# A broadcast matmul issued one projection unit later, and VectorE's next low weights ahead of the copy of its result

## Chip, cores, metric

The kernel runs on one core of a Trainium2 chip. The metric is the device time of one execution in microseconds; lower is better. The core's engines are TensorE (PE; its weight loads are listed as PEld), VectorE (DVE), ScalarE (ACT), GpSimd (POOL), and SyncE (SP), which here issues the DMAs.

## What is computed

One decoder layer on x (2 x 256 x 512, float32): attention with 32 heads of 128, a product with a quantised context, and a feed-forward part with a low-rank mixture. Only the attention's projections matter here:

```python
q = hidden_states @ Wq + bq
k = hidden_states @ Wk + bk
v = hidden_states @ Wv + bv
q = rms_norm(q, gq)      # over all 4096 columns, before the heads are split
k = rms_norm(k, gk)
...
attn = softmax(einsum('bhqd,bhkd->bhqk', q, k) / sqrt(128))
```

`rms_norm(x, w)` is `w * x * rsqrt(mean(x*x) + 1e-6)`. The mean runs over the 4096 columns of one token, so no key can be normalised until all 32 heads of keys are projected.

## The kernel before

The 512 tokens (T) stand along the free dimension, and the model's 512 columns lie in 4 chunks of 128 partitions. To keep float32's accuracy with TensorE's faster float32r matmuls, each operand is split into a high and a low part: the high part is a cast by ScalarE, the low part is the operand minus its high part. A product is three matmuls: high by high, low by high, high by low.

**Projection units.** One head of keys or queries is one unit. `project(i, r, before)` (line 476) is unit u = before + 4i + r; keys are units 0 to 31 (before = 0), queries units 32 to 63 (before = NH = 32). A unit is 12 matmuls (4 chunks by 3) of 128x512 into one of two PSUM banks: `p_flat[2]` (the profile calls it p_t) for even units, `p_flat[3]` (p_o) for odd ones. It waits for its low weights (`w_lo_dve`, line 480) and, for its bank, until the squares of the unit two before are taken (line 482).

**The feeding of a unit.**
- SyncE loads the head's weights into one of four slots of `raw` (line 322) once `w_lo_dve` says that the slot is free.
- ScalarE casts them to `w_hi` (`weights_hi`, line 695). There are two weight buffers, so it waits until unit u - 2 is finished (`proj_ready`, line 694). Then it takes a finished unit out of PSUM (`take`): with its bias into `k_all` or `q_all` (line 709), and squared into `square` (line 710).
- VectorE makes `w_lo` = `raw` - `w_hi` (`weights_lo`, line 1080).
- GpSimd adds the squares into `acc_k` or `acc_q` (`add_square`, line 929).

**The norms of the keys.** After unit 33 TensorE sums `acc_k` over the partitions with eight small matmuls (`sum_squares`, line 501) into `p_flat[0]` (p_v). VectorE scales them (`mean_squares`, line 1156), GpSimd takes the power -0.5 into `rk_t` (line 937). VectorE writes four diagonal tiles `diag` (line 1164), and TensorE multiplies `ones` with them (line 524) into `p_flat[1]` (p_s), which puts every token's factor on all partitions. VectorE copies this to `rkb` (line 1167). Then `norm_k` (line 1085) multiplies each head of `k_all` by its gain and by `rkb`.

**The order of the work** is the order of the instructions written out for each engine; every engine works through its own list, and semaphores hold it at the waits. VectorE's list around the change: `weights_lo` for units 32, 33, 34; `mean_squares`; the four `diag`; `weights_lo` for unit 35; the wait for `rkb_ready` and the copy to `rkb`; then, for units 36 to 39, `weights_lo` and two `norm_k` behind each (head r and head 4 + r); from unit 40 on one `norm_k` for each unit. TensorE's list: units 32 and 33, `sum_squares`, unit 34, the wait for `diag_made` and the broadcast matmul, unit 35, then a loop over units 36 to 63.

Behind the projections stands a loop over 16 pairs of heads: scores, softmax, the values' projection and the output projection, woven together in the same way; behind it the quantised product and the feed-forward part.

Of the kernel before, what the change touches and what calls it, by code (L numbers as in the profile page):

```python
# [33 lines left out]
NH, DH = 32, 128  # L34
# [14 lines left out]
def decoder_layer(nc, x, ctx_t, wk, wq, wv, wo, bk, bq, bv, bo, gk, gq, qscal, ra_w, base_b, router_b, bm_w,  # L49
                  expert_map, out):  # L50
    st = ExitStack()
    with st:
        def sem(name):
            return st.enter_context(nc.semaphore(name))
# [18 lines left out]
        def here(name, shape, dt, at=None):  # L73
            return place(name, shape, dt, at)[0]
# [50 lines left out]
        rkb = here("rkb", [P, T], F32, vl_at + half)  # L125
# [60 lines left out]
        p_flat = [p_v[:].rearrange("p a b -> p (a b)"), p_s[:].rearrange("p a b -> p (a b)"),  # L186
                  p_t[:].rearrange("p a b -> p (a b)"), p_o[:]]
# [22 lines left out]
        rkb_ready = sem("rkb_ready")  # L210
# [73 lines left out]
        def peeled(n, first, end):  # L284

            return isinstance(n, int) and first <= n < end

        def head(a, h):

            return a[:, bass.ds(h, 1), :].rearrange("p a t -> p (a t)")  # L290

        def column(a, h):
            return a[:, bass.ds(h, 1)]

        def parts(n):

            return [w[:, n, 0:NC * DH].rearrange("p (c n) -> p c n", c=NC) for w in (w_hi, w_lo)]
# [165 lines left out]
        def _(pe):  # L463
# [12 lines left out]
            def project(i, r, before):  # L476

                u = before + 4 * i + r
                n = r % 2
                pe.wait_ge(w_lo_dve, u + 1)  # L480
                if not peeled(u, 0, 2):
                    pe.wait_ge(squared, u - 1)
                hi, lo = parts(n)
                for c in range(NC):
                    pe.matmul(p_flat[2 + n], hi[:, c, :], xnt_hi[:, c, :], start=(c == 0), stop=False)  # L485
                    pe.matmul(p_flat[2 + n], lo[:, c, :], xnt_hi[:, c, :], start=False, stop=False)  # L486
                    if not peeled(u, 0, 1):
                        mm = pe.matmul(p_flat[2 + n], hi[:, c, :], xnt_lo[:, c, :], start=False,  # L488
                                       stop=(c == NC - 1))
                if peeled(u, 0, 1):  # L490
                    pe.wait_ge(xt_lo, NT)
                    for c in range(NC):
                        mm = pe.matmul(p_flat[2 + n], hi[:, c, :], xnt_lo[:, c, :], start=False,
                                       stop=(c == NC - 1))
                mm.then_inc(proj_ready, 1)

            def sum_squares(sums, dst, n):

                pe.wait_ge(summed, n)
                for t in range(NT):  # L500
                    mm = pe.matmul(dst[:, t:t + 1], sums[:, t * P:(t + 1) * P], ones[:, 0:1],
                                   start=True, stop=True)
                mm.then_inc(ssq_ready, 1)
# [7 lines left out]
            for r in range(4):  # L511
                pe.wait_ge(xb_lo_done, r + 1)
                for part in (xb_hi, xb_lo):
# [6 lines left out]
            project(0, 1, NH)  # L520
            sum_squares(acc_k, p_flat[0], NH)
            project(0, 2, NH)
            pe.wait_ge(diag_made, NT)
            pe.matmul(p_flat[1], ones[:], diag[:].rearrange("p t n -> p (t n)"), start=True, stop=True
                      ).then_inc(rkb_ready, 1)
            project(0, 3, NH)
            with pe.Fori(1, NH // 4) as i:
                for r in range(4):
                    project(i, r, NH)
# [491 lines left out]
        def _(dve):  # L1021
            links = 0

            def link(ins):

                nonlocal links
                links += 1
                ins.then_inc(chain, 1)
                dve.wait_ge(chain, links)
# [47 lines left out]
            def weights_lo(i, r, before):  # L1077
                dve.wait_ge(w_hi_done, before + 4 * i + r + 1)
                n = r % 2
                dve.tensor_tensor(w_lo[:, n, 0:NC * DH], raw[:, r, :], w_hi[:, n, 0:NC * DH], ALU.subtract  # L1080
                                  ).then_inc(w_lo_dve, 1)

            def norm_k(i, r):
                h = 4 * i + r
                dve.scalar_tensor_tensor(out=head(k_all, h), in0=head(k_all, h), scalar=column(g_c, h),
                                         in1=rkb[:], op0=ALU.mult, op1=ALU.mult).then_inc(k_normed, 1)
# [76 lines left out]
            for t in range(NT):  # L1163
                dve.tensor_scalar(diag[:, t, :], ident[:], rk_t[:, t:t + 1], None, ALU.mult).then_inc(diag_made, 1)
            weights_lo(0, 3, NH)
            dve.wait_ge(rkb_ready, 1)
            link(dve.tensor_copy(rkb[:], p_flat[1]))
            for r in range(4):
                weights_lo(1, r, NH)
                norm_k(0, r)  # L1170
                norm_k(1, r)
            with dve.Fori(2, NH // 4) as i:
# [289 lines left out]
```

## Time and profile before

| | us |
|---|---|
| median of 3 runs | 540.79 |
| the runs | 540.56, 540.79, 543.37 |
| the profiled execution, its own time | 541.91 |
| its span, first to last instruction | 540.1 |

Busy time of the engines in that span: TensorE 524.2 us (97%), ScalarE 355.6 (66%), VectorE 330.3 (61%), GpSimd 269.9 (50%). Times inside the profile are counted from the start of the span. The profiled execution took 1.8 us more than its span, and 1.1 us more than the median of the runs. In a row of a timeline stand the start, the duration, engine, line, operation, output<-inputs, shape and count; in brackets the idle time of the engine before it and what ended it.

### The profile page before, as it was taken

Reading aid. Unit: us, or ns where it says so; the run is one execution under the profiler, and the core shown is the slowest. Engines: PE = TensorE matmul, PEld = TensorE weight load, DVE = VectorE, ACT = ScalarE, POOL = GpSimd, SP = SyncE. Lnnn points to the kernel's source line nnn. Section 1 sums busy time; section 2 is a strip of 40 time slices with the busy share of each in tenths; the row PEclk is TensorE's granted clock in tenths of the full one; section 3 lists DMA queues with packets and bytes.
Section 4 is the critical chain, followed back from the end, with each engine's and each line's share of the span. In section 5 each row is a group of like instructions: output and inputs, shape, how many; then the busy total and the mean of one; then the engine's idle time right before and its main releaser. Section 6 shows DMA issues by size and latency. Waiting matters only on the chain.

```text
span 540.1 us, 9859 instructions
## 1 busy us (share of the span) xinstructions
PE 524.2 (97%) x3246; PEld 464.5 (86%) x3246; DVE 330.3 (61%) x695; ACT 355.6 (66%) x745; POOL 269.9 (50%) x229
## 2 busy tenths in 40 slices
PE   6999999989999999999999999999999999999887
PEld 6888888868888889999999999999999999986486
DVE  6254444287555567666766666666666666666665
ACT  3566666546666667767777777767767776776730
POOL 3344444355444446564646555464646556465340
PEclk9999999999999999999999999999999999999999
DMA  5344735323333321222122111121142311220002
GB/s 181 130 138 130 231 94 172 97 60 97 97 97 97 78 80 41 58 60 59 58 58 58 51 53 51 58 58 58 58 120 65 124 50 57 59 79 19 1 1 79
DMA packets 23351, 43.43 MB, mean 80 GB/s; under 512 B 3616, under 2 KB 3616, under 8 KB 23072
## 3 DMA queue, kind: packets, MB, share of 16 engines
q1 hardware_dynamic: 23328, 43.13, 26.7%
q8 instruction: 13, 0.21, 0.2%
q14 instruction: 10, 0.08, 0.0%
HBM read 41.03 MB, written 2.10 MB: 80 GB/s over the span
## 4 chain that ended last, share of the span: by engine, by line
PE 72%; issue 9%; POOL 8%; DVE 5%; ACT 3%; DMA 1%; POOLq 0%; SPq 0%; ACTq 0%; DVEq 0%
POOL acc_k L929 7%; PE p_v L564 5%; PE p_v L566 5%; PE p_v L565 5%; PE acc L583 5%; PE acc L584 5%; PE acc L585 5%; PE p_t L550 5%; PE p_o L602 3%; PE p_o L604 3%; PE p_o L486 3%; PE p_o L603 3%; PE p_o L485 3%; PE p_o L488 3%; PE p_s L543 3%
## 5 line engine op out<-in xcount | busy, mean ns | idle before, releaser
L1080 DVE TENSOR_TENSOR w_lo<-raw,w_hi 128x512 fp32r<-128x512 f32 x64 | 44.2, 691 | 82.1 <-ACT w_hi L695 82.1
L947 POOL TENSOR_TENSOR wo_lo<-raw,wo_hi 128x512 fp32r<-128x512 f32 x31 | 40.0, 1290 | 100.2 <-ACT wo_hi L829 100.2
L695 ACT CAST w_hi<-raw 128x512 fp32r<-128x512 f32 x64 | 39.9, 623 | 70.0 <-PE p_o L488 32.8
L764 ACT ACTIVATE probs<-p_s,nbias,rq_t 128x256 f32<-128x256 f32 x128 | 71.2, 562 | 19.2 <-DVE nbias L1182 19.2
L564 PE MATMUL p_v<-w_hi,xnt_hi 128*128 128x256 f32 x256 | 77.3, 302 | 0.0
L566 PE MATMUL p_v<-w_hi,xnt_lo 128*128 128x256 f32 x256 | 72.3, 283 | 0.0
L565 PE MATMUL p_v<-w_lo,xnt_hi 128*128 128x256 f32 x256 | 72.3, 282 | 0.0
L929 POOL TENSOR_TENSOR acc_k<-acc_k,square 128x512 f32<-128x512 f32 x32 | 41.6, 1300 | 53.5 <-ACT square L710 53.5
L929 POOL TENSOR_TENSOR acc_q<-acc_q,square 128x512 f32<-128x512 f32 x32 | 42.7, 1334 | 43.1 <-ACT square L710 42.8
L813 ACT CAST pt_hi<-p_t 128x512 fp32r<-128x512 f32 x64 | 37.3, 583 | 38.4 <-PE p_t L550 38.4
L947 POOL TENSOR_TENSOR w_lo<-raw,w_hi 128x512 fp32r<-128x512 f32 x32 | 44.9, 1404 | 20.6 <-ACT w_hi L747 20.6
L1180 DVE TENSOR_REDUCE nmax<-p_s 128x2 f32<-128x512 f32 x64 | 43.9, 686 | 14.5 <-PE p_s L543 13.6
L485 PE MATMUL p_t<-xnt_hi,w_hi 128*128 128x512 f32 x128 | 50.1, 391 | 0.7 <-ACT xnt_hi L719 0.7
L583 PE MATMUL acc<-wo_hi,o_hi 128*128 128x512 f32 x124 | 49.4, 398 | 1.0 <-POOL wo_lo L947 0.6
L485 PE MATMUL p_o<-xnt_hi,w_hi 128*128 128x512 f32 x128 | 50.2, 392 | 0.0
L486 PE MATMUL p_t<-xnt_hi,w_lo 128*128 128x512 f32 x128 | 49.9, 390 | 0.0
L488 PE MATMUL p_o<-xnt_lo,w_hi 128*128 128x512 f32 x128 | 49.8, 389 | 0.0
L486 PE MATMUL p_o<-xnt_hi,w_lo 128*128 128x512 f32 x128 | 49.8, 389 | 0.0
L564 PEld LDWEIGHTS p_v<-w_hi,xnt_hi 128*128 128x128 f32 x256 | 48.8, 191 | 0.3 <-issue 0.2
L584 PE MATMUL acc<-wo_hi,o_lo 128*128 128x512 f32 x124 | 49.0, 395 | 0.0
L565 PEld LDWEIGHTS p_v<-w_lo,xnt_hi 128*128 128x128 f32 x256 | 48.9, 191 | 0.0
L566 PEld LDWEIGHTS p_v<-w_hi,xnt_lo 128*128 128x128 f32 x256 | 48.7, 190 | 0.0
(263 smaller groups left out, 1500.9 us busy)
## 6 DMA issues: line engine op xcount, KB each, us to landing
raw<-in_wv SPq DMA_DIRECT2D x36, 256.0 KB, 2.6
raw<-in_wk SPq DMA_DIRECT2D x32, 256.0 KB, 2.6
raw<-in_wq SPq DMA_DIRECT2D x32, 256.0 KB, 2.6
raw<-in_wo SPq DMA_DIRECT2D x31, 256.0 KB, 2.6
ctx_f<-in_ctx SPq DMA_DIRECT2D x4, 512.0 KB, 3.6
xin<-in_x SPq DMA_DIRECT2D x4, 256.0 KB, 3.7
xb<-in_x SPq DMA_DIRECT2D x4, 256.0 KB, 5.9
ctx_kept<-ctx_k SPq DMA_DIRECT2D x1, 1024.0 KB, 5.0
```

Source lines behind the costliest of these rows:

```text
L485: pe.matmul(p_flat[2 + n], hi[:, c, :], xnt_hi[:, c, :], start=(c == 0), stop=False)
L486: pe.matmul(p_flat[2 + n], lo[:, c, :], xnt_hi[:, c, :], start=False, stop=False)
L488: mm = pe.matmul(p_flat[2 + n], hi[:, c, :], xnt_lo[:, c, :], start=False, stop=(c == NC - 1))
L564: pe.matmul(p_v[:, t % 2, :], xnt_hi[:, c, tt], hi[:, c, :], start=(c == 0), stop=False)
L565: pe.matmul(p_v[:, t % 2, :], xnt_hi[:, c, tt], lo[:, c, :], start=False, stop=False)
L566: mm = pe.matmul(p_v[:, t % 2, :], xnt_lo[:, c, tt], hi[:, c, :], start=False, stop=(c == NC - 1))
L583: pe.matmul(acc[t][:], oh[:, tt], wh[:], start=False, stop=False, skip_group_check=True)
L584: pe.matmul(acc[t][:], ol[:, tt], wh[:], start=False, stop=False, skip_group_check=True)
L764: act.activation(probs[:, b, a, :], p_s[:, a, :], ACT.Exp, bias=nbias[:, b, a:a + 1], scale=rq_t[:, 2 * b + a:2 * b + a + 1], accum_out=rs ...
L929: pool.tensor_tensor(sums[:], sums[:], square[:, r % 2, :], ALU.add).then_inc(summed, 1)
L947: pool.tensor_tensor(dst, raw[:, slot, :], hi, ALU.subtract).then_inc(w_lo_pool, 1)
L1080: dve.tensor_tensor(w_lo[:, n, 0:NC * DH], raw[:, r, :], w_hi[:, n, 0:NC * DH], ALU.subtract).then_inc(w_lo_dve, 1)
```

## The change

TensorE issues unit 35 (`project(0, 3, NH)`) ahead of the wait for the diagonal tiles and the broadcast matmul, instead of behind them. VectorE makes the low weights of unit 36 ahead of the wait for the broadcast matmul's result and of its copy, instead of behind them. The first two `norm_k` stay behind the copy. All else is as it was, VectorE's order of `diag` and the low weights of unit 35 included.

```diff
@@ -520,10 +520,10 @@
             project(0, 1, NH)
             sum_squares(acc_k, p_flat[0], NH)
             project(0, 2, NH)
+            project(0, 3, NH)
             pe.wait_ge(diag_made, NT)
             pe.matmul(p_flat[1], ones[:], diag[:].rearrange("p t n -> p (t n)"), start=True, stop=True
                       ).then_inc(rkb_ready, 1)
-            project(0, 3, NH)
             with pe.Fori(1, NH // 4) as i:
                 for r in range(4):
                     project(i, r, NH)
@@ -1163,10 +1163,11 @@
             for t in range(NT):
                 dve.tensor_scalar(diag[:, t, :], ident[:], rk_t[:, t:t + 1], None, ALU.mult).then_inc(diag_made, 1)
             weights_lo(0, 3, NH)
-            dve.wait_ge(rkb_ready, 1)
-            link(dve.tensor_copy(rkb[:], p_flat[1]))
             for r in range(4):
                 weights_lo(1, r, NH)
+                if r == 0:
+                    dve.wait_ge(rkb_ready, 1)
+                    link(dve.tensor_copy(rkb[:], p_flat[1]))
                 norm_k(0, r)
                 norm_k(1, r)
             with dve.Fori(2, NH // 4) as i:
```

## Rows read from the trace of the kernel before

**Rows 1.** The page: TensorE's busy time, the chain's shares, the query weights' DMAs

```profile
PE 524.2 (97%) x3246; PEld 464.5 (86%) x3246; DVE 330.3 (61%) x695; ACT 355.6 (66%) x745; POOL 269.9 (50%) x229
...
PE 72%; issue 9%; POOL 8%; DVE 5%; ACT 3%; DMA 1%; POOLq 0%; SPq 0%; ACTq 0%; DVEq 0%
...
raw<-in_wq SPq DMA_DIRECT2D x32, 256.0 KB, 2.6
```

**Rows 2.** Windows: length, busy (count) of PE, PEld, DVE, ACT, POOL; clock, DMA, GB/s

```profile
116.00:190.00 74.00, 74.00 (x328) 61.31 (x327) 42.56 (x58) 49.54 (x84) 35.91 (x27) 1.00 0.33 92
206.00:510.00 304.00, 300.29 (x2136) 275.95 (x2134) 205.11 (x466) 220.72 (x513) 168.12 (x138) 1.00 0.20 60
```

**Rows 3.** TensorE's timeline: broadcast, unit 35's first matmuls, starts of units 36 and 37

```profile
112.28 1.13 PE L524 MATMUL p_s<-diag,ones 128*128 128x512 f32 x2 [1.41 <-DVE diag L1164]
112.88 0.75 PE L485 MATMUL p_o<-xnt_hi,w_hi 128*128 128x512 f32 x1
113.47 0.40 PE L486 MATMUL p_o<-xnt_hi,w_lo 128*128 128x512 f32 x1
...
116.00 0.39 PE L485 MATMUL p_t<-xnt_hi,w_hi 128*128 128x512 f32 x1
...
118.72 0.39 PE L485 MATMUL p_o<-xnt_hi,w_hi 128*128 128x512 f32 x1
```

**Rows 4.** VectorE's timeline, from the diagonals to the low weights of unit 38 and the norms behind

```profile
109.31 2.91 DVE L1164 TENSOR_SCALAR diag<-ident,rk_t 128x128 f32<-128x128 f32 x4 [1.14 <-POOL rk_t L937]
112.14 0.68 DVE L1080 TENSOR_TENSOR w_lo<-raw,w_hi 128x512 fp32r<-128x512 f32 x1
113.44 0.69 DVE L1167 COPY rkb<-p_s 128x512 f32<-128x512 f32 x1 [0.62 <-PE p_s L524]
114.17 0.69 DVE L1080 TENSOR_TENSOR w_lo<-raw,w_hi 128x512 fp32r<-128x512 f32 x1
114.78 1.41 DVE L1085 SCALAR_TENSOR_TENSOR k_all<-k_all,g_c,rkb 128x512 f32<-128x512 f32 x2
116.86 0.69 DVE L1080 TENSOR_TENSOR w_lo<-raw,w_hi 128x512 fp32r<-128x512 f32 x1 [0.67 <-ACT w_hi L695]
117.47 2.45 DVE L1085 SCALAR_TENSOR_TENSOR k_all<-k_all,g_c,rkb 128x512 f32<-128x512 f32 x2
119.84 0.68 DVE L1080 TENSOR_TENSOR w_lo<-raw,w_hi 128x512 fp32r<-128x512 f32 x1
120.44 2.44 DVE L1085 SCALAR_TENSOR_TENSOR k_all<-k_all,g_c,rkb 128x512 f32<-128x512 f32 x2
```

**Rows 5.** Waits of the weight loads, 106 to 131 us (total, times, longest)

```profile
PEld p_o L485 <- DVE w_lo L1080: 0.3, 1, 0.3
```

**Rows 6.** TensorE's timeline: the first three matmuls after an idle spell elsewhere

```profile
204.14 0.35 PE L602 MATMUL p_o<-pt_hi,v_hi 128*128 128x256 f32 x1 [0.64 <-DVE pt_lo L1249]
204.33 0.28 PE L603 MATMUL p_o<-pt_hi,v_lo 128*128 128x256 f32 x1
204.45 0.28 PE L604 MATMUL p_o<-pt_lo,v_hi 128*128 128x256 f32 x1
```

**Rows 7.** ScalarE's timeline: the high weights of units 35, 36 and 37

```profile
107.28 0.62 ACT L695 CAST w_hi<-raw 128x512 fp32r<-128x512 f32 x1 [0.93 <-PE p_o L488]
...
110.90 0.62 ACT L695 CAST w_hi<-raw 128x512 fp32r<-128x512 f32 x1 [1.83 <-PE p_t L488]
...
116.20 0.62 ACT L695 CAST w_hi<-raw 128x512 fp32r<-128x512 f32 x1 [3.52 <-PE p_o L488]
```

**Rows 8.** GpSimd's timeline: the squares of units 35 and 36

```profile
118.06 1.30 POOL L929 TENSOR_TENSOR acc_q<-acc_q,square 128x512 f32<-128x512 f32 x1 [4.03 <-ACT square L710]
120.86 1.47 POOL L929 TENSOR_TENSOR acc_q<-acc_q,square 128x512 f32<-128x512 f32 x1 [1.50 <-ACT square L710]
```

**Rows 9.** Lines 1216 and 1217: count, duration in ns (min/median/max), first and last start

```profile
L1216 DVE TENSOR_TENSOR k_lo<-k_all,k_hi x1: 684/684/684, 191.5 to 191.5; 128x512 fp32r<-128x512 f32 x1
L1217 DVE TENSOR_TENSOR q_lo<-q_all,q_hi x1: 1783/1783/1783, 192.1 to 192.1; 128x512 fp32r<-128x512 f32 x1
```

## The prediction, made before the change was run

> **What bounds the kernel now.** I read the page first: TensorE (PE) is busy for 524.2 us of a span of 540.1, and it has by far the largest share of the chain that ended last [rows 1]. So a microsecond that TensorE loses is a microsecond of the span, unless a later wait swallows it. The windows say where such a wait could be: from 116 to 190 us TensorE is busy for all 74.00 us, and from 206 to 510 us for 300.29 of 304 [rows 2]. The rest of the kernel is fed by TensorE's own results, so nothing downstream has a date of its own; I take it that a delay at 116 us goes through to the end whole.
>
> Next I read TensorE's timeline around the edit [rows 3]. I number projection units from 0: units 0 to 31 are keys, 32 to 63 queries; `project(0,2,NH)` is unit 34 and `project(0,3,NH)` unit 35. After unit 34 TensorE idles 1.41 us until the diagonal tiles are made, and at 112.28 the broadcast matmul (line 524) starts, recorded as two of 1.13 us together. Unit 35 is issued at 112.88, but its second matmul follows only at 113.47, one pitch of 0.23 after the first really streams; so the first streams at 113.24. From there unit 36 begins 2.76 later, at 116.00, and units follow each other by 2.72 (116.00, 118.72). That 1.41 us is the only idle time that the edit can aim at.
>
> Then the other queues. VectorE makes the four diagonal tiles from 109.31 to 112.22 and, **behind them**, the low weights of unit 35 from 112.14 to 112.82 [rows 4]. The waits of the weight loads show one of 0.3 us, unit 35's, and it is for these low weights [rows 5]: they are ready just when TensorE asks, and no earlier.
>
> **What the change does, part by part.**
>
> *The broadcast matmul goes behind unit 35.* The wait for the diagonals leaves the front of unit 35. But unit 35 waits for w_lo of unit 35, and the diff leaves VectorE's order of diagonals, then w_lo(35), untouched. The wait does not go away; what is late next is w_lo(35). TensorE starts at 112.88 instead of 112.28 (from end of w_lo at 112.82 the 0.06 us seen before). The same matmuls are issued behind either start: one broadcast and unit 35, which took 116.00 − 112.28 = 3.72 us. So unit 36 starts at 112.88 + 3.72 = 116.60: **+0.60 us**. In other words the broadcast matmul used to run beside VectorE's w_lo(35), and loses that cover. Should the order matter for the matmul's price, 112.28 to 113.24 bounds it at 0.96 us with the restart; a restart costs some 0.07 (after an idle spell the first two matmuls start 0.19 apart, the next 0.12 [rows 6]), so I take 0.89 in mid-stream, between 0.8 and 1.1, the term moving with it between +0.5 and +0.8.
>
> *VectorE's w_lo(36) ahead of the copy.* It was made from 114.17 to 114.86 and needed at 116.00 [rows 3, 4]. Now it is made before the copy, with the high weights cast at 110.90 [rows 7]. It had 1.1 us of slack, so its gain is nothing. Without this edit it would sit behind the late copy, and that would cost; it only keeps its cover.
>
> *What now queues behind the late result.* The broadcast starts at 116.60 − 0.89 = 115.71. The copy used to start 1.16 after a start from idle, so 1.09 without the restart: 116.80. On VectorE, behind this wait, stand the copy, two norm_k and then w_lo(37), which unit 37 needs. Before, w_lo(37) was made at 116.86 ahead of its own two norms and needed at 118.72. Now: copy 116.80, first norm 0.73 later at 117.53, the second 0.66 later. If nothing disturbed them, w_lo(37) would run from 118.85 to 119.53, and TensorE, through with unit 36 at 116.60 + 2.72 = 119.32, would wait for 0.34 with signal and restart.
>
> They are disturbed. Two norms took 1.41 us at 114.78 and 2.45 at 117.47, where GpSimd's sum of squares ran from 118.06 to 119.36; the norms ended 0.56 after it [rows 4, 8]. At 120.44 the same again: GpSimd starts at 120.86, ends 1.14 after the first norm, at 122.33, and the second norm ends 0.55 later. So they take turns, whole instructions at a time. The subtraction at line 1217, of the same form as w_lo (a tensor minus another, both in SBUF), took 1783 ns where its neighbour at line 1216 took 684 [rows 9]. The Trainium skill, GPSIMD Engine Reference, Key points, says that GpSimd shares its SBUF interfaces with VectorE and contends with VectorE instructions that have two SBUF inputs. The trace agrees; norms and w_lo are all of that kind.
>
> Where is GpSimd now? ScalarE's cast of the high weights starts 0.20 after a unit ends, and GpSimd 1.86 after the cast (116.20 and 118.06) [rows 7, 8]. Unit 35 ends at 115.71, cast 115.91, GpSimd at 117.77, inside the first norm (117.53 to 118.28). GpSimd takes the next turn and ends at 119.42, the second norm at 119.98, w_lo(37) runs from 119.90 to 120.58, and unit 37 starts at 120.71 (0.06 and 0.07 more) instead of 119.32: **+1.39 us**. If GpSimd wins the first turn, all end the same.
>
> *The next round.* Unit 38 is wanted at 123.43. Norms at 120.50 and 121.16 to 121.91; unit 36 ended at 119.32, so GpSimd comes at 121.38, inside the second norm, and ends at 121.91 + 1.14 = 123.05. w_lo(38) ends at 123.61, unit 38 starts at 123.74: **+0.31 us**. It is nothing if VectorE keeps the turn. For w_lo(39) the cast waits for unit 37 (ends 123.43), GpSimd comes at 125.49, and w_lo(39), from 124.86 to 125.54, is ahead of it and needed at 126.46. From unit 40 on there is one norm per unit, and the delay stops growing.
>
> *Queues passed.* No DMA is moved. The load into the raw slot that w_lo(37) frees is issued 3 us later (120.6 for 117.5); it takes 2.6 us [rows 1] and is cast for unit 41 only when unit 39 ends, near 129.2. Cover of 6 us.
>
> **Sum:** 0.60 + 1.39 + 0.31 = 2.30 us. The profiled execution took 541.91 us with its span of 540.1; the sum on it gives 544.2. It stands 1.1 above the median of the runs, 540.79; on that, 543.1 us, 0.43% slower. About 0.5% (2.7 us) is what a measurement of this kernel can tell from no change.
>
> **The rivals.**
>
> *No turns taken, or fewer.* For it: w_lo itself has never met GpSimd in the projection loops, and the second turn rests on 0.2 us of timing. Then the terms are 0.60 + 0.34, or the third is nothing: 0.9 to 2.0 us, 541.7 to 542.8. Against it: both norms of rows 4 were held each time. Chance 0.24.
>
> *A third round: slower by over 0.5%.* VectorE's queue is fuller than TensorE's in units 37 to 39: w_lo(37) and w_lo(38) were made 2.98 us apart before (116.86, 119.84 [rows 4]) against units of 2.72, so it loses ground each round. If GpSimd's turn falls ahead of w_lo(39) instead of behind it, that ends at 126.77 + 0.56 = 127.33 and unit 39 starts at 127.46 for 126.46: one us more, 3.3 in all, 544.1. It decides where w_lo(39) starts after 125.49; I have it 0.6 earlier. Chance 0.18.
>
> *The change does what it says.* Unit 35 starts behind unit 34 and the 1.41 us go. It needs w_lo(35) made by 110.87, where the 1.41 us of idle time begin. Its high weights are cast by 107.9 [rows 7], so it could have been; but it stands behind the diagonals in the program, and VectorE works in order. The gain would be 1.41, 539.4, still within 0.5%. Chance 0.04.
>
> **How the numbers follow.** Forecast 0.54, rivals 0.24, 0.18, 0.04. The range 541.3 to 544.4 takes in the small case nearly whole and the third round. Within 0.5%: 0.54 + 0.24 + 0.04 = 0.82, of which 0.02 go to slower (the broadcast at its upper bound) and 0.01 to faster, so 0.79; slower 0.18 + 0.02 = 0.20; faster 0.01.
>
> **What would show it.** In the changed profile: TensorE idle about 2 us before unit 35, released by w_lo and not by the diagonals; the broadcast behind unit 35; VectorE's copy near 116.8; a second wait for w_lo of about 1.3 us before unit 37 and perhaps a third, small, before unit 38; norms of 1.78 us beside GpSimd's sums. The forecast is wrong if unit 35 starts near 110.9, if unit 37 starts without a wait, or if waits go on after unit 38; and also if TensorE's granted clock falls below the full value it holds throughout now [rows 2].

## The result, and the profile after

The changed kernel takes 544.86 us in the median of 14 runs (542.81 to 548.59), the kernel before 541.54 in the median of 14 (540.52 to 543.98). The ratio is 1.0063 with a 95% interval of 1.0041 to 1.0085: slower, by about 3.3 us. The forecast was a ratio of 1.0043 (2.30 us, 543.1), likeliest within 0.5%, with a range that ended at 544.4. So the direction was right and the size too small by 1 us. The median lies outside the range by 0.5 us. Of its distance to the forecast, 0.75 us come from the median of before, now 541.54 for 540.79: counted from the new median, the range would end at 545.15 and hold the result. The ratio does not depend on that, and it is above the 0.5% within which the forecast had it.

The profiled execution took 544.50 us with a span of 542.7. TensorE's timeline around the change (the lines that answer to [rows 3]); units 34 and 35, the broadcast, and the first matmuls of units 36 to 39:

```profile
106.38 0.49 PE L485 MATMUL p_t<-xnt_hi,w_hi 128*128 128x512 f32 x1
...
111.42 0.50 PE L485 MATMUL p_o<-xnt_hi,w_hi 128*128 128x512 f32 x1 [2.01 <-DVE w_lo L1080]
111.76 0.39 PE L486 MATMUL p_o<-xnt_hi,w_lo 128*128 128x512 f32 x1
...
112.74 0.63 PE L488 MATMUL p_o<-xnt_lo,w_hi 128*128 128x512 f32 x1
113.17 0.63 PE L485 MATMUL p_o<-xnt_hi,w_hi 128*128 128x512 f32 x1
...
115.72 1.17 PE L525 MATMUL p_s<-diag,ones 128*128 128x512 f32 x2
116.33 0.79 PE L485 MATMUL p_t<-xnt_hi,w_hi 128*128 128x512 f32 x1
...
120.84 0.49 PE L485 MATMUL p_o<-xnt_hi,w_hi 128*128 128x512 f32 x1 [1.23 <-DVE w_lo L1080]
...
123.80 0.50 PE L485 MATMUL p_t<-xnt_hi,w_hi 128*128 128x512 f32 x1
...
126.67 0.39 PE L485 MATMUL p_o<-xnt_hi,w_hi 128*128 128x512 f32 x1
```

The first wait is now 2.01 us, in front of unit 35, and what ends it is w_lo and not the diagonals. The second, of 1.23, stands in front of unit 37. Unit 38 begins 0.32 after the last matmul of unit 37 was issued at 123.48, instead of 0.23: the third, small one. All three were forecast. But look at the durations within unit 35. They are 0.39 at first and 0.63 from the sixth matmul on, and the starts stand 0.43 apart where they stood 0.23. The windows say why (columns as in [rows 2]):

```profile
109.40:111.40 2.00, 0.01 (x1) 0.00 (x0) 2.00 (x4) 1.78 (x3) 1.18 (x2) 1.00 0.00 0
111.40:112.40 1.00, 0.98 (x4) 0.85 (x5) 0.57 (x1) 0.00 (x0) 1.00 (x1) 1.00 0.00 0
112.40:115.70 3.30, 3.30 (x9) 2.52 (x9) 0.00 (x0) 0.00 (x0) 0.71 (x1) 0.53 0.56 159
115.70:117.00 1.30, 1.30 (x5) 0.75 (x4) 0.07 (x1) 1.04 (x2) 0.00 (x0) 0.88 0.00 0
```

From 112.4 to 115.7 TensorE's granted clock is 0.53 of full, that is, the lower level of 1.2 GHz nearly all the time. Finer windows put the fall at 112.6, 1.2 us **after** the idle spell, while TensorE was busy again, and the return at 116.0, some 3.4 us later. The Trainium skill, TensorE: Matmul & The Clock Gate, Part 1, says that the chip gates TensorE's clock to half according to how busy the engine has been; the trace agrees.

VectorE's timeline (for [rows 4]) and GpSimd's (for [rows 8]) show the turns:

```profile
107.86 2.91 DVE L1164 TENSOR_SCALAR diag<-ident,rk_t 128x128 f32<-128x128 f32 x4 [1.14 <-POOL rk_t L937]
110.69 1.28 DVE L1080 TENSOR_TENSOR w_lo<-raw,w_hi 128x512 fp32r<-128x512 f32 x2
116.94 0.69 DVE L1170 COPY rkb<-p_s 128x512 f32<-128x512 f32 x1 [4.96 <-PE p_s L525]
117.66 2.45 DVE L1085 SCALAR_TENSOR_TENSOR k_all<-k_all,g_c,rkb 128x512 f32<-128x512 f32 x2
120.04 0.68 DVE L1080 TENSOR_TENSOR w_lo<-raw,w_hi 128x512 fp32r<-128x512 f32 x1
120.64 1.40 DVE L1085 SCALAR_TENSOR_TENSOR k_all<-k_all,g_c,rkb 128x512 f32<-128x512 f32 x2
121.96 1.78 DVE L1080 TENSOR_TENSOR w_lo<-raw,w_hi 128x512 fp32r<-128x512 f32 x1
```

```profile
117.83 1.74 POOL L929 TENSOR_TENSOR acc_q<-acc_q,square 128x512 f32<-128x512 f32 x1 [4.71 <-ACT square L710]
121.60 1.60 POOL L929 TENSOR_TENSOR acc_q<-acc_q,square 128x512 f32<-128x512 f32 x1 [2.03 <-ACT square L710]
```

VectorE is idle 4.96 us for the broadcast. Then the two norms cost 2.45 beside GpSimd's sum, w_lo(37) ends at 120.72, and TensorE goes on at 120.84. In the next round it is w_lo(38) itself that is held, 1.78 us for 0.68: a w_lo had never met GpSimd in the projection loops of before, and it is held as line 1217 was.

**How the delay adds up.** The starts of the two executions differ (unit 34 began at 107.84 before and at 106.38 now, since the first unit began 1.4 us earlier), so I measure from the start of unit 34. To the start of unit 39 it was 124.16 − 107.84 = 16.32 us; now it is 126.67 − 106.38 = 20.29, 3.97 more. The forecast has 2.30 of it. Eight matmuls from 112.46 to 115.72 took 3.26 us for 8 x 0.227 = 1.81, so 1.45 more, and the broadcast some 0.1 more: the clock has the rest.

The 14 runs say the same. Those with a mean granted clock of 1.000 took 542.81, 543.17 and 543.17 us; at 0.996 to 0.997 the runs took 543.7 to 544.9, at 0.993 up to 545.7, at 0.987 to 0.990 548.0 to 548.6. A mean does not say where in the kernel the clock was low; the traces below show two more places.

### The profile page after: what moved, and what is told of

It is laid out like the page before. It is cut to its first block, busy times and chain, and to the rows that moved or that the text cites. A ratio compares the mean times of both kernels' runs of the same rounds, so it can differ in the third digit from the quotient of the medians.

```text
span 542.7 us, 9856 instructions
## 1 busy us (share of the span) xinstructions
PE 524.9 (97%) x3244; PEld 464.1 (86%) x3246; DVE 329.0 (61%) x695; ACT 355.6 (66%) x745; POOL 271.0 (50%) x229
## 4 chain that ended last, share of the span: by engine, by line
PE 71%; issue 9%; POOL 8%; DVE 6%; ACT 3%; DMA 1%; POOLq 0%; SPq 0%; ACTq 0%; DVEq 0%
POOL acc_k L929 7%; PE p_v L564 5%; PE p_v L566 5%; PE p_v L565 5%; PE acc L583 5%; PE acc L584 5%; PE acc L585 5%; PE p_t L550 5%; PE p_o L485 3%; PE p_o L488 3%; PE p_o L602 3%; PE p_o L486 3%; PE p_o L604 3%; PE p_o L603 3%; PE p_s L543 3%
## 5 line engine op out<-in xcount | busy, mean ns | idle before, releaser
L1080 DVE TENSOR_TENSOR w_lo<-raw,w_hi 128x512 fp32r<-128x512 f32 x64 | 45.3, 709 | 81.7 <-ACT w_hi L695 81.7
L929 POOL TENSOR_TENSOR acc_q<-acc_q,square 128x512 f32<-128x512 f32 x32 | 43.8, 1370 | 45.9 <-ACT square L710 45.6
```

The costliest lines, as they stand in the source:

```text
L929: pool.tensor_tensor(sums[:], sums[:], square[:, r % 2, :], ALU.add).then_inc(summed, 1)
```

## The experiments

The yardstick in the traces is the time from the start of unit 34 to the start of unit 41, 21.76 us before (129.60 − 107.84), or to unit 39, 16.32. It leaves the start and the tail of the kernel out.

**The changed kernel again**, on another chip, as it is:

> The changed kernel once more, beside the two above on the same chip. My account: its fastest runs, at clock 1.000, at 543.1 us (before + 2.3); the others, at 0.987 to 0.997, up to 5 us more; median 544.5 to 545. Rival, that the earlier runs were a property of their chip: median at 543 and no low clocks.

Median 544.59 us of 6 runs (543.55 to 545.04), ratio 1.0058 (1.0035 to 1.0080), 3.5 us above the 541.07 of before beside it. One run had clock 1.000, with 543.55. Its profile fell on a run in which the clock held in this stretch, and so shows the queue's part alone: TensorE waits 2.01 and 1.18 us, and unit 41 begins 24.14 us after unit 34, **2.38 more than before, against 2.30 forecast**. The trace with the fallen clock has 20.29 to unit 39, this one 18.70: 1.59 us for one fall of the clock.

```profile
111.48 0.50 PE L485 MATMUL p_o<-xnt_hi,w_hi 128*128 128x512 f32 x1 [2.01 <-DVE w_lo L1080]
...
114.34 1.02 PE L525 MATMUL p_s<-diag,ones 128*128 128x512 f32 x2
...
119.30 0.49 PE L485 MATMUL p_o<-xnt_hi,w_hi 128*128 128x512 f32 x1 [1.18 <-DVE w_lo L1080]
```

**The idle spell filled.** Eight matmuls with nothing to do, in front of unit 35; their bank is overwritten by the broadcast:

```diff
             project(0, 2, NH)
+            for _ in range(8):
+                pe.matmul(p_flat[1], ident_r[:], xnt_hi[:, 0, :], start=True, stop=True)
             project(0, 3, NH)
```

> The changed kernel, with 8 matmuls of 128x512 put into TensorE's idle spell of 2.0 us before unit 35 (8 x 0.227 = 1.8 us, results overwritten by the broadcast). Theory that the missing 1.5 us are TensorE's clock, fallen to half after that spell: the granted clock is 1.000 in nearly all runs, unit 35's matmuls stay at 0.39 us, the spread of runs shrinks, and the time is before + 2.3 us (ratio 1.004). Rival, that the runs above 543.2 us come from elsewhere (the start, the loads): same median and spread as the changed kernel, ratio 1.006.

Median 543.33 us of 12 runs, all of them between 542.97 and 543.79; ratio 1.0035 (1.0020 to 1.0050). Of the 20 runs of the changed kernel in the two sets above 14 took more than 544.4. The wait before unit 37 is still there, and unit 41 begins 24.13 us after unit 34.

```profile
109.26 1.98 PE L524 MATMUL p_s<-xnt_hi,ident_r 128*128 128x512 f32 x8
111.46 0.50 PE L485 MATMUL p_o<-xnt_hi,w_hi 128*128 128x512 f32 x1 [0.23 <-DVE w_lo L1082]
...
119.29 0.49 PE L485 MATMUL p_o<-xnt_hi,w_hi 128*128 128x512 f32 x1 [1.18 <-DVE w_lo L1082]
```

Work that serves nothing makes the changed kernel 1.5 us faster in the median. What it removes is idle time alone. The spread goes from 5.8 us to 0.8, though not all of that is due to this place: the three slowest of the 14 runs lost more than a fall here costs, and they are taken up at the end. The clock holds in this stretch of the trace:

```profile
111.40:117.00 5.60, 5.54 (x22) 4.24 (x23) 2.20 (x5) 1.79 (x3) 2.39 (x2) 1.00 0.28 94
117.00:121.00 4.00, 2.82 (x12) 1.99 (x11) 4.00 (x5) 1.78 (x3) 1.92 (x2) 1.00 0.16 31
```

Over the whole run seven of the 12 had clock 1.000, two 0.999 and three 0.996 to 0.997, so "nearly all" was too much. The profiled one, at 0.996, shows where: the clock falls once near the end, 1.6 us after another idle spell has ended.

```profile
515.00 0.65 PE L429 MATMUL acc<-ident,xn 128*128 128x128 f32 x4 [1.46 <-ACT xn L874]
```

```profile
516.70:520.00 3.30, 3.30 (x18) 3.30 (x17) 2.53 (x9) 0.81 (x1) 1.35 (x3) 0.50 0.00 0
```

All 13 traces of this document have that spell of 1.46 us, with the same work around it. In ten the clock held, the kernel before among them. In three it fell: here, in the changed kernel again, and in the run with w_lo(37) ahead of the copy. From the spell's end to the end of the span the ten take 26.2 to 26.3 us and the three 26.7 to 26.8, so a fall there costs some 0.5 us.

**The spell made longer without the change.** The kernel before, with w_lo(35) between the wait for the power and the diagonals:

```diff
             dve.wait_ge(rms_done, 1)
+            weights_lo(0, 3, NH)
             for t in range(NT):
                 dve.tensor_scalar(diag[:, t, :], ident[:], rk_t[:, t:t + 1], None, ALU.mult).then_inc(diag_made, 1)
-            weights_lo(0, 3, NH)
```

> The kernel before in TensorE's order, with w_lo(35) between the wait for the power and the diagonals, so that the diagonals come later and TensorE's idle spell in front of the broadcast grows from 1.41 to some 2.0 to 2.7 us; nothing else of the change is in it. Theory that the length of this idle spell brings the clock down: runs under clock 1.000 become the rule as in the changed kernel, and the median is 1 to 2 us above what the longer spell alone gives (+0.6 to +1.3 us). Rival, that the clock falls for another reason of the changed kernel (the second wait, or unit 35 first): clocks and spread as before, and the time is before + 0.6 to 1.3 us.

Median 542.88 us of 12 runs (541.23 to 546.24), ratio 1.0026 (1.0008 to 1.0044). The idle spell in front of the broadcast became 2.07 us. Of six runs at clock 1.000 five took 541.2 to 541.8, some 0.5 above before, as the longer spell asks; five at 0.997 took 543.0 to 544.4, and the worst at 0.991 546.2. Neither the share of runs under 1.000 (6 of 12, and 15 of 29 of before beside it) nor the median, whose interval takes in the longer spell alone, tells the two accounts apart. What such a run costs does: those of before at 0.996 and 0.997 took 541.0 to 542.1. In the trace the clock falls again, 0.7 us after the work resumes at 111.62, and unit 41 begins 24.01 us after unit 34, 2.25 more than before. The longer spell is 0.66 of it (2.07 for 1.41), which leaves 1.59 for the clock, the same as in the changed kernel.

```profile
109.40:111.60 2.20, 0.15 (x1) 0.00 (x0) 2.17 (x5) 1.79 (x3) 1.65 (x2) 1.00 0.29 101
111.60:113.00 1.40, 1.38 (x3) 0.63 (x4) 0.00 (x0) 0.00 (x0) 1.12 (x1) 0.75 0.08 28
113.00:116.00 3.00, 3.00 (x9) 2.37 (x8) 2.71 (x4) 0.00 (x0) 0.00 (x0) 0.55 0.03 8
116.00:118.00 2.00, 2.00 (x10) 1.65 (x9) 0.20 (x1) 0.86 (x2) 0.00 (x0) 1.00 0.34 128
```

There is no second wait here and unit 35 does not come first, so the rival falls: neither is needed for the clock to fall behind a spell of 2.0 us.

**The spell of before filled**, with six matmuls:

```diff
             project(0, 2, NH)
+            for _ in range(6):
+                pe.matmul(p_flat[1], ident_r[:], xnt_hi[:, 0, :], start=True, stop=True)
             pe.wait_ge(diag_made, NT)
```

> The kernel before with 6 matmuls of 128x512 in its idle spell of 1.41 us (6 x 0.227 = 1.36 us). Theory that idle time of TensorE in this place brings the clock down in some runs of before too: its runs at 0.993 to 0.997 clock with 543 to 544 us go, and the median stays at 541 within 0.3 us. Rival, that those runs of before come from another place: as many of them as before.

Median 541.08 us, ratio 0.9998 (0.9982 to 1.0014): nothing. One of 12 runs still took 543.92 at clock 0.994, as 3 of 23 runs of before did beside it (543.90 to 544.06). So at least some of the upper runs of before come from elsewhere, and this theory was wrong for them; 12 runs are too few to say how many. A trace of such a run (below, norms spread) shows where.

**VectorE's half alone**, TensorE's order as before:

> VectorE's half of the change alone: w_lo(36) ahead of the copy, TensorE's order as before. My account: the broadcast still starts 112.28 after the same idle spell of 1.41 us, w_lo(36) was never late, so the time is that of before within 0.5 us; the copy may come up to 1.1 us later (w_lo(36) meets GpSimd's sum at 112.76) with no one waiting for it. The granted clock stays at 1.000 as before. A rival, that the later norms alone cost TensorE a wait, expects a wait for w_lo of some tenths at unit 37 or 38 and +0.3 to +1 us.

Median 540.96 us, ratio 1.000 (0.9982 to 1.0017). Unit 41 begins 21.77 us after unit 34, as before. w_lo(36) and the copy trade places and nobody waits; the whole loss is TensorE's half.

**TensorE's half alone**, VectorE's order as before:

> TensorE's half alone: unit 35 ahead of the broadcast, VectorE copies ahead of w_lo(36). My account: idle 2.0 us before unit 35 as in the changed kernel (+0.60), then w_lo(36) behind the copy ends some 0.7 us after it, so unit 36 waits about 1.7 us from the broadcast's end, and the norms behind it shift w_lo(37) to about the same place relative to unit 37 or better; total +3 to +5 us without the clock, and more where the granted clock is under 1.000. The rival, that the cost of the change does not come from VectorE's queue, expects it at the changed kernel's time, +3.3 us.

Median 544.76 us of 9 runs (543.23 to 548.64), ratio 1.0068 (1.0040 to 1.0097). The trace shows 2.01 us before unit 35 and 1.59 before unit 36, now for w_lo(36) behind the copy; unit 41 begins 24.49 after unit 34, 2.73 more than before. That is just under the 3 to 5 us that I expected: past unit 36 there was no further wait, since the one wait of 1.59 also gave VectorE the time for w_lo(37).

```profile
111.73 0.50 PE L485 MATMUL p_o<-xnt_hi,w_hi 128*128 128x512 f32 x1 [2.01 <-DVE w_lo L1080]
...
117.20 0.49 PE L485 MATMUL p_t<-xnt_hi,w_hi 128*128 128x512 f32 x1 [1.59 <-DVE w_lo L1080]
```

So VectorE's half did keep a cover, as forecast, worth some 0.35 us by the traces (24.49 for 24.14). The medians cannot tell this from the rival, which expected the changed kernel's time: 544.76 here and 544.86 there.

**w_lo(35) ahead of the diagonals**, in the changed kernel:

```diff
             mean_squares(p_flat[0], 1)
+            weights_lo(0, 3, NH)
             dve.wait_ge(rms_done, 1)
             for t in range(NT):
                 dve.tensor_scalar(diag[:, t, :], ident[:], rk_t[:, t:t + 1], None, ALU.mult).then_inc(diag_made, 1)
-            weights_lo(0, 3, NH)
```

> The changed kernel, with w_lo(35) made ahead of the diagonals, in VectorE's idle 1.1 us while GpSimd takes the power. Theory that the wait only moved to w_lo(35): unit 35 follows unit 34 without idle time, the broadcast runs from 113.4 to 114.3 on the clock of the trace before, which is 1.7 us earlier than before for unit 36; the wait for w_lo(37) of about 1.3 us and a small one for w_lo(38) stay. Sum -1.7 + 1.4 + 0.3 = 0.0, the time of before within 0.5 us where the clock stays at 1.000. Rival, that unit 35 is held by something else than w_lo(35) (its bank, the squares): the 2.0 us idle spell stays and the time is the changed kernel's.

Median 541.10 us, ratio 0.9993 (0.9974 to 1.0013), as summed. The first idle spell is gone, the second stands at 1.18 us, and unit 41 begins 21.79 after unit 34 (21.76 before). So w_lo(35) alone held unit 35, and one line that was not in the change decides whether the change gains anything.

**The same line in the kernel before:**

> The kernel before, with w_lo(35) ahead of the diagonals in VectorE's idle 1.1 us. My account: the broadcast still waits for the diagonals, idle 1.41 us as before, and nothing gets faster: 541.1 us within 0.5. Rival, that the earlier w_lo alone is worth the gain: -0.6 us or more.

Median 541.34 us, ratio 1.0013 (0.9998 to 1.0028); unit 41 begins 22.16 after unit 34, 0.40 later than before. It is a small loss, within the noise of the median, and the idle spell is 1.80 us where I expected 1.41, for w_lo(35) now runs beside GpSimd's power, which takes 1.40 us for 1.02 and makes the diagonals late. The line helps only with TensorE's new order, in which no one waits for the diagonals.

**w_lo(37) ahead of the copy**, in the changed kernel, by making every low weight one step earlier:

```diff
             weights_lo(0, 3, NH)
+            weights_lo(1, 0, NH)
             for r in range(4):
-                weights_lo(1, r, NH)
+                if r < 3:
+                    weights_lo(1, r + 1, NH)
                 if r == 0:
```

> The changed kernel, with w_lo(37) ahead of the wait for the broadcast's result too, and each later w_lo one step ahead of its two norms. My account: the wait before unit 37 (1.2 us and restart) and the small one before unit 38 go, since w_lo(37) can be made while the broadcast runs; the 2.0 us idle spell before unit 35 stays with its +0.6 us and its clock. Runs at clock 1.000: about 541.5 us; the others 1.5 us and more above. Rival, that TensorE would wait at unit 37 anyway for its bank or for ScalarE's cast: the wait stays and the fastest runs stand at 543.

Median 545.12 us of 6 runs (543.65 to 545.73), ratio 1.0062 (1.0043 to 1.0081). Neither account fits. The wait before unit 37 is gone, but TensorE's waits (weight loads left out) name a new one, of 1.8 us for w_lo(40), and VectorE's timeline shows it:

```profile
PE p_o L485 <- DVE w_lo L1080: 2.0, 1, 2.0
PE p_t L485 <- DVE w_lo L1080: 1.8, 1, 1.8
```

```profile
124.20 4.82 DVE L1085 SCALAR_TENSOR_TENSOR k_all<-k_all,g_c,rkb 128x512 f32<-128x512 f32 x4
128.94 0.68 DVE L1080 TENSOR_TENSOR w_lo<-raw,w_hi 128x512 fp32r<-128x512 f32 x1
```

My edit left four norms in a row at the end of the group. With GpSimd's sums in between (at 124.47 and 127.19) they take 4.82 us, more than a unit. The edit moved the wait from one unit to another. The fastest run, 543.65, is near the 543 that the rival named, but not for its reason. The profiled run, at 0.993, had two falls of the clock, at 112.9 and at 519.1.

**Both edits together:**

> The changed kernel with w_lo(35) ahead of the diagonals and w_lo(37) ahead of the copy. My account: both new waits go, and the idle 1.41 us of the kernel before with them; TensorE runs units 34, 35, the broadcast, units 36 and 37 without idle time; unit 36 starts 1.7 us earlier than before, and that stays to the end: 539.4 us, ratio 0.997, granted clock 1.000 in this stretch. Rival, that GpSimd's turns make some other w_lo of units 38 to 40 late: a wait of some tenths to 1.3 us there, 540 to 541 us.

Median 541.68 us, ratio 1.0018 (1.0005 to 1.0032). To unit 39 it is 14.65 us, 1.67 less than before, and then the same four norms make unit 40 wait 1.75. The rival of this run was right in kind, a late w_lo at unit 40, though 1.75 us and 541.7 are more than the 1.3 us and 541 that it allowed; the place was my own making.

**The norms spread.** Both edits, and behind the copy two norms or one between a w_lo and the next (the lines taken out are not shown, nor w_lo(35), which stands ahead of the wait for the power):

```diff
+            weights_lo(1, 0, NH)
+            weights_lo(1, 1, NH)
+            dve.wait_ge(rkb_ready, 1)
+            link(dve.tensor_copy(rkb[:], p_flat[1]))
+            head_n = 0
+            for u, norms in zip(range(5, 12), (2, 1, 2, 1, 2, 2, 2)):
+                if u > 5:
+                    weights_lo(u // 4, u % 4, NH)
+                for _ in range(norms):
+                    norm_k(head_n // 4, head_n % 4)
+                    head_n += 1
+            with dve.Fori(3, NH // 4) as i:
```

> w_lo(35) ahead of the diagonals, w_lo(37) ahead of the copy, and behind the copy two norms or one between one w_lo and the next (2, 1, 2, 1, 2, 2, 2), never the four in a row of e7_both, which made w_lo(40) 1.75 us late. My account: no wait for w_lo is left in the projections, unit 36 starts 1.7 us earlier than before and that stays: 539.4 us, ratio 0.997. Rival, that the queue of VectorE cannot keep up with two norms and GpSimd's turns at 2.72 us a unit in this stretch, wherever they stand: a wait of 0.3 to 1.5 us at one of units 38 to 44, 540 to 541 us.

Median 539.52 us of 12 runs (539.02 to 541.74), ratio **0.9964 (0.9949 to 0.9978)**: faster than both kernels, by 1.5 us than before. Unit 41 begins 20.09 after unit 34, 1.67 less than before, and TensorE has no wait from 104 to 196 us. The gain is only clear with an interval; it is under 0.5%.

```profile
112.14 0.39 PE L485 MATMUL p_o<-xnt_hi,w_hi 128*128 128x512 f32 x1
...
114.86 1.02 PE L525 MATMUL p_s<-diag,ones 128*128 128x512 f32 x2
115.32 0.80 PE L485 MATMUL p_t<-xnt_hi,w_hi 128*128 128x512 f32 x1
```

The profiled run was its slowest, 541.74 at clock 0.994, and its windows show where such a run loses:

```profile
6.00:12.00 6.00, 3.94 (x22) 3.10 (x20) 5.59 (x17) 2.67 (x5) 2.81 (x5) 0.76 0.56 186
12.00:18.00 6.00, 5.65 (x17) 4.52 (x18) 1.97 (x4) 1.66 (x4) 0.00 (x0) 0.67 0.26 79
18.00:24.00 6.00, 6.00 (x28) 4.96 (x27) 1.98 (x4) 4.19 (x8) 2.57 (x2) 1.00 0.49 142
```

It is at the start, where TensorE has gaps while x lands and is normalised. From 6 to 12 us it is busy for 3.94 us here; in the traces of before and of the changed kernel, in which the clock held, it is busy for 5.08 and 4.55. After its first matmuls its longest listed wait is 1.39 us here, up to 7.97, and 0.81 and 0.68 us there. The kernel before has the same instructions at the start. That its runs at 0.994 (543.6 to 544.3 us, some 3 above those at full clock) lose there too is likely by this one trace, and not shown for each.

## Why the prediction was wrong, by its own steps

- **That the wait only moves**: right. Unit 35 waits 2.01 us for w_lo(35) (about 2 forecast), and w_lo(35) ahead of the diagonals takes that wait away.
- **The broadcast loses its cover, +0.60**: right. From the start of unit 34 to where unit 36 streams was 8.16 us before (116.00 − 107.84). In the trace of the changed kernel at full clock the second matmul of unit 36 starts at 115.43, so the first streams one pitch earlier, at 115.20: 8.76 us after 106.44, 0.60 more.

- **w_lo(36) earlier gains nothing**: right for the kernel before (ratio 1.000), and its cover is worth some 0.35 us in the new order.
- **Turns with GpSimd, +1.39 and +0.31**: right in size, 1.18 to 1.23 us of idle time and the restart for the first, and a w_lo(38) held 1.78 us for the second. All three terms together measured 2.38 for 2.30.
- **The delay goes to the end whole**: right. With the idle spell filled it is 2.37 us in the trace (24.13 for 21.76) and 2.2 in the medians.
- **The step that failed** is the sum, which counts every microsecond of idle time as one microsecond. "TensorE's granted clock falls below the full value" stands among the things that would make the forecast wrong, but it had no price and no chance. It was the rival to work out. The idle spell grew from 1.41 to 2.0 us, and that it ran at full clock so far was shown for the shorter one alone, in one trace. Measured, one fall costs 1.59 us (20.29 for 18.70 to unit 39), and with the spell filled the median drops by 1.5.
- **The rival that named a third round** did not happen: w_lo(39), made at 125.00, came ahead of GpSimd's turn at 125.77. That a measured time over 0.5% got its chance of 0.20 from there was luck in the number, and not in the reason.

What stays open: where the runs of the changed kernel that lose 5 us (clock 0.987 to 0.990) lose it. No trace caught one. An estimate from the three places that traces show fits them: the full-clock 543.1 us, 1.6 for the fall here, some 3 for the start and some 0.5 for the place near the end give 547.7 without the last and 548.2 with it. The mean clocks would be 0.991 and 0.987, by the 0.997, 0.994 and 0.996 of the traces with one fall each. The runs took 548.0 at 0.990 and 548.3 and 548.6 at 0.987. A fall behind the second idle spell is not excluded. Open too is why the same spell brings the clock down in one run and not in another.

## What to carry to other kernels

Before a waiting step is moved behind another, look at what the other one waits for and where that stands in its own engine's list: here both came from VectorE, and the second stood behind the first. A late result is paid again by all that queues behind its wait, so put work with a date (w_lo) ahead of the wait and spread work without one (the norms) thinly. And price idle time of TensorE twice: once for its length, once for the clock, by comparing it with the longest spell that the trace shows at full clock in the same surroundings. One trace is not enough for that: 1.46 us near the end held in ten traces here and did not in three, so look at the granted clock of many runs.

## What the runs showed that I had not expected

- A spell of 2.0 us without work in a stretch in which TensorE was otherwise always busy brought its clock to half for some 3.4 us, starting 0.7 to 1.4 us after the work resumed, in the traces of three kernels (the changed one, the longer spell, w_lo(37) ahead) and not in those of two others with the same spell (the changed one again, TensorE's half). So it is a matter of the run. Spells of 1.41 or 1.18 us in the same place left the medians where the sums put them; one of 1.80 us (w_lo(35) ahead, in the kernel before) ran at full clock in its trace. Near the end 1.46 us were enough in three traces of 13.
- Where VectorE's two instructions follow each other closely, it may keep the turn: w_lo(35) and w_lo(36), back to back, took 1.28 us, and GpSimd's sum, due between them, took 1.81 for 1.27. Against line 1080 at 121.96 GpSimd won. Even a 128x4 operation of GpSimd, the power, stretches so, from 1.02 to 1.40 us beside w_lo(35).
